# Cross-attention and a ternary feed-forward block on one core: single PE transposes between long matmuls in place of blocks of four and eight

## The chip, the core and the metric

The kernel is one program on one core of a Trainium2 chip. It has five engines with a queue each: TensorE (PE: matmuls, and PEld, its weight loads), VectorE (DVE), ScalarE (ACT), GpSimd (POOL) and SyncE (SP, which only issues DMAs here). An engine runs its queue in the order in which the program lists it. The metric is the time of one execution on the device in microseconds (us); lower is better.

## The reference

Eight sequences of 256 tokens with 512 features go through two residual blocks. What is computed, cut to what matters:

```python
q, k, v = heads(layernorm(x) @ Wq.T + bq), heads(ctx @ Wk.T + bk), heads(ctx @ Wv.T + bv)   # 16 heads of 32
q1, k1 = relu(q @ Wqf.T), relu(k @ Wkf.T) * mask            # 64 features for each head
out = (q1 @ (k1.T @ v)) / (q1 @ k1.sum(tokens) + 1e-8)      # linear attention
x = x + out @ Wo.T + bo
y = layernorm(x)                                            # int8-like rounding by row: bit_linear
a = bit_linear(y, w_up) * relu(bit_linear(y, w_gate)) ** 2  # ternary weights, 512 -> 2048
x = x + bit_linear(rmsnorm(a) * g, w_down)                  # 2048 -> 512
```

## The kernel before, in words

Two kinds of tile are used. A sequence a (0 to 7) has two row tiles i = 2a and 2a+1 of 128 tokens each. The attention part is computed in pairs of numbers: a high part in the matmul format fp32r (`.hi`, written by ACT) and the rest as a low part (`.lo`, written by DVE), so each product takes three matmuls: high*high, high*low and low*high. The feed-forward part runs in bf16 on small integers.

First comes the context part: keys, values and features of all eight sequences, up to about 160 us. Then a loop over p = 0 to 5 with a = p+1 and n = p+2 interleaves the feed-forward of row tiles 2p and 2p+1 with the attention of sequence a and with the start of sequence n, and a word list, TAIL, does the same for the end. The work of one turn, in the order in which PE gets it:

- `s3(a)`: feature matmuls of the queries. `gate_up(i, h)`: 8 gate and 8 up matmuls of 128x512 in bf16 for one half of the hidden width. `down(i)`: 16 matmuls of 128x512 in bf16.
- `s4(a, t)`: the attention product, 24 small matmuls (`at`, 66 columns) for each of the two row tiles. `mix(main, side, lag, end)` deals these 48 small ones out between the long matmuls of `gate_up` and `down`. It leaves the first `lag` and the last `end` long ones alone. Where there are more small ones than gaps, some gaps get two or more.
- `s5(a, t)`: the normalised attention output of a row tile (in `xn`) is transposed on PE: four fp32 transposes of 128x128, named `oT`, through a PSUM bank. ACT copies the high part into `qoh`, DVE the low part into `qol`. For t = 0 this stands in the side list of `mix` as one entry, for t = 1 behind the mix.
- `s6(a, t)`: the output projection of a row tile, 12 matmuls of 128x512 (`pr`, reading `qoh` or `qol` and `woh` or `wol`), then by DVE the residual sum (`x1`) and the layernorm statistics, then rounding (`xm`, `am`, `xq`), and a DMA that transposes the rounded tile into `xqT`, which `gate_up` of that tile reads in the next turn.
- `s1(n, t)`: four PE transposes of the normalised input of the next sequence (`xT`); ACT writes the high part into `aph` (`xT.hi`), DVE the low part into `apl` (`xT.lo`). `s2(n)`: 48 query matmuls of 128x256 that read `aph` and `apl` of both row tiles. The first of them waits for both `xT.lo`.

Only PE's order is written by hand. `Plan.queues` sorts the queues of ACT, DVE, POOL and SP: it runs through the program with a table of costs, and each free engine takes the open step with the smallest of (due time, need); a step's need is reckoned back from PE's order. So another order on PE also gives other orders on ACT, DVE, POOL and SP. Nothing is reordered on the chip: an ACT or DVE instruction waits behind what stands ahead of it.

The lines that matter: L338 emits all matmuls, L589 the transposes, L341 the ACT operations, L344 and L350 DVE operations. In `ps<-woh,qoh` the first name behind the arrow is the streamed operand and the second the loaded one.

Of the kernel before, what the change touches and what calls it, by code (L numbers as in the profile page):

```python
# [224 lines left out]
def xattn_bitffn_kernel(nc, x_d, ctx_d, wk_d, wv_d, wq_d, wo_d, feat_d, small_d, bv_d, bo_d, g_d, wg_d, wu_d, wd_d, out_d):  # L225
# [4 lines left out]
    with ExitStack() as es:  # L230
# [354 lines left out]
        def transposes(tag, t, waits):  # L585
            b = bank()
            for kc in range(KC):
                out, src = ps[:, b, P * kc:P * kc + P], xn[:, t, P * kc:P * kc + P]
                add("pe", f"{tag}.{kc}", 0.11, (waits + bank_user[b] + ["small"]) if kc == 0 else [], lambda e, out=out, src=src: e.transpose(out, src, eye))  # L589
            return b, f"{tag}.3"  # L590

        def s1(a, t):
            i = 2 * a + t
            b, k = transposes(f"xT{i}", t, [f"xn{i}"])
            src = ps[:, b, :].rearrange("p (a c) -> p a c", a=KC)

# [96 lines left out]
        def s5(a, t):  # L693
            i = 2 * a + t
            tt("pool", f"xbo{i}", 1.23, [f"xn{i}", "bo"], xs[:, i, :], xs[:, i, :], bo_b[:, :], ALU.add)
            b, k = transposes(f"oT{i}", t, [f"on{i}.0", f"on{i}.1"])
            cs = slice(512 * t, 512 * t + 512)
            act(f"oT{i}.hi", 0.5, [k], qoh[:, cs], ps[:, b, :], ACT.Copy)
            bank_user[b] = [tt("dve", f"oT{i}.lo", 0.62, [k, f"oT{i}.hi"], qol[:, cs], ps[:, b, :], f32(qoh[:, cs]), ALU.subtract)]
# [4 lines left out]
        def s6(a, t):  # L704
            i = 2 * a + t
            b = bank()
            for kc in range(KC):
                cs = slice(512 * t + P * kc, 512 * t + P * kc + P)
                waits = [f"oT{i}.lo"] + Wo_lo + bank_user[b] if kc == 0 else []
                k = products(f"pr{i}.{kc}", 0.2138, waits, ps[:, b, :], (qoh[:, cs], qol[:, cs]), (woh[:, kc, :], wol[:, kc, :]), kc == 0, kc == KC - 1)  # L710
            bank_user[b] = [tt("dve", f"x1.{i}", 0.62, [k, f"xbo{i}"], xs[:, i, :], ps[:, b, :], xs[:, i, :], ALU.add)]
# [185 lines left out]
        s6(0, 0)  # L897
        s1(1, 0)
        s1(1, 1)
        s6(0, 1)  # L900
        s2(1)
        kv_blocks(1)

# [102 lines left out]
```

How the kernel before makes its waits and increments, by code:

```python
        def run(lane, eng):  # L194
            seen = {}
            for i in order.get(lane, []):
                _, name, _, waits, fn, dma = self.steps[i]
                need = {}
                for w in waits:
                    s, v = at[w]
                    if need.get(s, (0, None))[0] < v:
                        need[s] = (v, w)
                for s, (v, _) in need.items():
                    if seen.get(s, 0) < v:
                        eng.wait_ge(s, v)
                        seen[s] = v
                last = fn(eng)
                if dma is not None:
                    last.then_inc(dma_sems[dma], 16)
                elif name in at:
                    last.then_inc(sems[lane], 1)
# [6 lines left out]
        def sync(e):  # L218
            run("sp", e)
            e.wait_ge(dma_sems["out"], issued["out"])
```

## Time and profile before

| | us |
|---|---|
| median of 3 runs (lowest, highest) | 475.62 (475.36, 476.45) |
| the profiled execution | 473.81 |
| its span, first to last instruction | 472.0 |
| PE busy | 460.8 (98%) |
| DVE busy | 359.2 (76%) |
| ACT busy | 301.9 (64%) |
| POOL busy | 178.5 (38%) |

PE is busy through nearly the whole span. The recorded time of a matmul runs from its dispatch to its last result, so neighbours overlap in the record: what a matmul costs is read from start to start, not from its duration. Of a small matmul behind a long one the start is recorded early. The granted TensorE clock is full in all 40 slices of the page.

### The profile page before, as it was taken

The numbers are of one execution on the slowest core, as the hardware profiler recorded it, in microseconds if no ns is written. First come the engines' busy times: TensorE is split into PE (matmuls) and PEld (weight loads), VectorE is DVE, ScalarE is ACT, GpSimd is POOL, SyncE is SP. The second block draws the span as 40 slices with busy tenths as digits, with TensorE's granted clock in tenths as the row PEclk, the third lists the DMA queues.
The fourth block names the chain that finished last, engine by engine and source line by source line (L and its number), as shares of the span: only waits on it lengthen the run. The fifth ranks groups of instructions, "written<-read, shape, count | busy, mean of one in ns | idle before, by whom it ended". The sixth has DMA issues, their size and how long they took to land.

```text
span 472.0 us, 7966 instructions
## 1 busy us (share of the span) xinstructions
PE 460.8 (98%) x3059; PEld 367.9 (78%) x3059; DVE 359.2 (76%) x638; ACT 301.9 (64%) x441; POOL 178.5 (38%) x310
## 2 busy tenths in 40 slices
PE   8999999999999999999999999999999999998996
PEld 6899999999899997885786876777678678684443
DVE  4835658538994696897788789789779799878782
ACT  5682888638133327768578567684866686747991
POOL 0000000001530164753654646466364563553750
PEclk9999999999999999999999999999999999999999
DMA  8971463703600120015015113203301320432044
GB/s 258 422 313 44 177 226 110 292 1 115 242 2 0 31 83 22 3 44 135 24 44 124 35 44 80 62 19 81 98 24 44 90 46 10 114 78 58 12 111 135
DMA packets 53078, 45.49 MB, mean 96 GB/s; under 512 B 43440, under 2 KB 44336, under 8 KB 51120
## 3 DMA queue, kind: packets, MB, share of 16 engines
q1 hardware_dynamic: 53040, 44.98, 30.5%
q8 instruction: 24, 0.39, 0.4%
q14 instruction: 14, 0.11, 0.1%
HBM read 27.14 MB, written 4.19 MB: 66 GB/s over the span
## 4 chain that ended last, share of the span: by engine, by line
PE 73%; POOL 6%; DVE 6%; ACT 5%; DMA 4%; issue 3%; SPq 2%; POOLq 0%; DVEq 0%; ACTq 0%
PE ps L338 71%; POOL zb L344 3%; PE ps L589 2%; ACT rb L341 2%; DMA xs<-in_wq_dram 2%; SPq L335 2%; DMA xqT<-xqb 2%; DVE zb L344 1%; ACT zb L341 1%; POOL tk L344 1%; POOL tk L347 1%; DMA yqTq<-yqb 1%; DVE yqb L792 1%; POOL zbe L344 1%; POOL xs L344 0%
## 5 line engine op out<-in xcount | busy, mean ns | idle before, releaser
L344 POOL TENSOR_TENSOR zb<-zb,g_b 128x1024 f32<-128x1024 f32 x28 | 67.2, 2400 | 61.2 <-ACT rb L341 43.9
L338 PE MATMUL ps<-tg,xqT 128*128 128x512 bf16 x256 | 68.1, 385 | 2.8 <-DMA xqT<-xqb 2.7
L338 PE MATMUL ps<-tu,xqT 128*128 128x512 bf16 x256 | 68.2, 385 | 0.0
L341 ACT ACTIVATE qoh<-ps,small 128x256 fp32r<-128x256 f32 x64 | 27.9, 468 | 40.1 <-PE ps L338 40.0
L338 PE MATMUL ps<-td,yqT 128*128 128x512 bf16 x208 | 50.7, 384 | 0.0
L341 ACT ACTIVATE rb<-zb 128x1024 f32<-128x1024 f32 x29 | 30.7, 1059 | 25.3 <-DVE zb L344 25.1
L341 ACT ACTIVATE rb<-ps 128x1024 f32<-128x1024 f32 x29 | 29.6, 1022 | 24.8 <-PE ps L338 23.8
L344 DVE TENSOR_TENSOR zb<-ps,rb 128x1024 f32<-128x1024 f32 x29 | 35.2, 1215 | 12.3 <-ACT rb L341 7.0
L341 ACT ACTIVATE zb<-zb,cm,tk 128x1024 f32<-128x1024 f32 x29 | 34.8, 1237 | 13.7 <-POOL tk L344 13.7
L338 PEld LDWEIGHTS ps<-tg,xqT 128*128 128x128 bf16 x256 | 23.8, 99 | 23.7 <-issue 2.9
L338 PEld LDWEIGHTS ps<-tu,xqT 128*128 128x128 bf16 x256 | 25.1, 99 | 21.5
L338 PE MATMUL ps<-kvh,apl 128*128 128x66 f32 x112 | 41.1, 367 | 0.0
L347 POOL TENSOR_SCALAR tk<-tk 128x1 f32<-128x1 f32 x96 | 30.7, 321 | 27.1 <-DVE tk L716 19.8
L338 PE MATMUL ps<-kvh,aph 128*128 128x66 f32 x112 | 40.2, 359 | 0.7 <-DVE apl L350 0.7
L338 PE MATMUL ps<-kvl,aph 128*128 128x66 f32 x112 | 40.4, 361 | 0.0
L765 DVE TENSOR_REDUCE tk<-zb 128x1 f32<-128x1024 f32 x30 | 36.3, 1210 | 3.3 <-POOL zb L344 3.2
L350 DVE SCALAR_TENSOR_TENSOR qol<-ps,small,qoh 128x256 fp32r<-128x256 f32 x64 | 27.9, 475 | 13.1 <-ACT qoh L341 12.9
L338 PE MATMUL ps<-aph,wkh 128*128 128x256 f32 x128 | 35.7, 283 | 0.7 <-DVE kp L347 0.7
L338 PE MATMUL ps<-aph,wqh 128*128 128x256 f32 x128 | 36.0, 281 | 0.1
L338 PE MATMUL ps<-apl,wqh 128*128 128x256 f32 x128 | 35.9, 280 | 0.0
L338 PE MATMUL ps<-aph,wql 128*128 128x256 f32 x128 | 35.9, 280 | 0.0
L338 PE MATMUL ps<-apl,wkh 128*128 128x256 f32 x128 | 35.3, 280 | 0.0
(153 smaller groups left out, 1357.0 us busy)
## 6 DMA issues: line engine op xcount, KB each, us to landing
xs<-in_wg_dram SPq DMA_DIRECT2D x4, 1024.0 KB, 13.4
xs<-in_wu_dram SPq DMA_DIRECT2D x4, 1024.0 KB, 5.3
xs<-in_wd_dram SPq DMA_DIRECT2D x4, 1024.0 KB, 9.3
xs<-in_x_dram SPq DMA_DIRECT2D x8, 512.0 KB, 4.1
out_dram<-xs SPq DMA_DIRECT2D x15, 256.0 KB, 2.0
craw<-in_ctx_dram SPq DMA_DIRECT2D x7, 512.0 KB, 7.4
qoh<-qol SPq DMA_DIRECT2D x12, 128.0 KB, 2.3
qy<-qol SPq DMA_DIRECT2D x12, 128.0 KB, 2.3
```

Source lines behind the costliest of these rows:

```text
L335: return add("sp", name, 2.9 * mb, waits, lambda e: e.dma_start(out, in_), sem)
L338: return add("pe", name, cost, waits, lambda e: e.matmul(out, lhsT, rhs, start=start, stop=stop))
L341: return add("act", name, cost, waits, lambda e: e.activation(out, in_, func, **kw))
L344: return add(lane, name, cost, waits, lambda e: e.tensor_tensor(out, a, b, op))
L347: return add(lane, name, cost, waits, lambda e: e.tensor_scalar(out, a, s1, s2, op0, op1))
L350: return add("dve", name, cost, waits, lambda e: e.scalar_tensor_tensor(out, a, s, b, op0, op1))
L589: add("pe", f"{tag}.{kc}", 0.11, (waits + bank_user[b] + ["small"]) if kc == 0 else [], lambda e, out=out, src=src: e.transpose(out, src, ...
L765: add("dve", f"ym{u}", 1.15, [f"Y{u}"], lambda e: e.tensor_reduce(col(M0 + h, i), zs, AX_X, ALU.max, apply_absolute_value=True))
L792: add("dve", f"yb{v}", 0.6, [f"yk{v}"] + war, lambda e, dst=dst, z=z: e.tensor_scalar(dst, z, MAGIC, None, ALU.subtract))
```

## The change

`transposes`, `s1`, `s5` and `s6` no longer emit their PE work at once: each gives back a list of calls, one for each transpose or matmul, with the copies and the row work behind the last one. The lists are dealt out by `mix`:

- The four transposes of `s5(a, 0)` are four entries in the side list of the attention products, where one entry stood before (52 in place of 49).
- In the loop the four transposes of `s1(n, 0)` are dealt out between the 12 projections of `s6(a, 0)`, and those of `s1(n, 1)` between the first five projections of `s6(a, 1)`.
- `s5(a, 1)`, and all of the sequences 0 and 1 ahead of the loop, keep their order. No instruction is added or left out.

```diff
-        def transposes(tag, t, waits):
-            b = bank()
+        def transposes(tag, t, waits, evict):
+            calls = []
+            cell = {}
             for kc in range(KC):
+                def call(kc=kc):
+                    if kc == 0:
+                        cell["b"] = bank()
+                    b = cell["b"]
...
+                    add("pe", f"{tag}.{kc}", 0.11, (waits + bank_user[b] + ["small"]) if kc == 0 else [], lambda e: e.transpose(out, src, eye))
+                    if kc == KC - 1:
+                        evict(b, f"{tag}.{kc}")
+                calls.append(call)
+            return calls
...
             side = s4(a, 0) + s4(a, 1)
-            side.insert(36, lambda: s5(a, 0))
+            side[36:36] = s5(a, 0)
             main = gate_up(2 * p, 1) + (down(2 * p - 1) if 0 < p < NB - 3 else []) + gate_up(2 * p + 1, 0) + gate_up(2 * p + 1, 1)
             mix(main, side, 6, 10)
-            s5(a, 1)
+            mix(s5(a, 1), [])
             ln1(n)
-            s6(a, 0)
-            s1(n, 0)
-            s1(n, 1)
-            s6(a, 1)
+            mix(s6(a, 0), s1(n, 0), 1, 3)
+            mix(s6(a, 1), s1(n, 1), 0, 8)
             s2(n)
...
                 side = s4(a, 0) + s4(a, 1)
-                side.insert(36, lambda: s5(a, 0))
+                side[36:36] = s5(a, 0)
                 mix(sum([part(w) for w in r.split(",")], []), side, 6, 10)
```

First place: PE between the bf16 matmuls, in the turn p = 4 (the list is `s4(5)` with `s5(5, 0)` in it). `tg`, `tu` mark gate and up matmuls, `kvh` and `kvl` the attention products, `small,xn` the transposes. Before:

```order
L338 MATMUL ps<-kvl,aph 128x66
L338 MATMUL ps<-tu,xqT 128x512
L338 MATMUL ps<-kvh,apl 128x66
L338 MATMUL ps<-tu,xqT 128x512
L589 MATMUL ps<-small,xn 128x128 x4
L338 MATMUL ps<-tu,xqT 128x512
L338 MATMUL ps<-kvh,aph 128x66
```

and in the changed kernel:

```order
L338 MATMUL ps<-tg,xqT 128x512
L595 MATMUL ps<-small,xn 128x128
L338 MATMUL ps<-tu,xqT 128x512
L595 MATMUL ps<-small,xn 128x128
L338 MATMUL ps<-tu,xqT 128x512
L595 MATMUL ps<-small,xn 128x128
L338 MATMUL ps<-tu,xqT 128x512
L595 MATMUL ps<-small,xn 128x128
L338 MATMUL ps<-kvh,aph 128x66
L338 MATMUL ps<-tu,xqT 128x512
```

Each transpose takes a gap of its own, or the first place of one, and the attention products that stood in these gaps move to others.

Second place: PE in the output projections of the same turn (`woh`, `wol`: `pr`). Before there were 12 projections, eight transposes and 12 projections; the rows around the eight:

```order
L338 MATMUL ps<-woh,qoh 128x512
L338 MATMUL ps<-wol,qoh 128x512
L338 MATMUL ps<-woh,qol 128x512
L589 MATMUL ps<-small,xn 128x128 x8
L338 MATMUL ps<-woh,qoh 128x512
```

In the changed kernel, from the first projection of the second row tile on:

```order
L338 MATMUL ps<-woh,qoh 128x512
L595 MATMUL ps<-small,xn 128x128
L338 MATMUL ps<-wol,qoh 128x512
L595 MATMUL ps<-small,xn 128x128
L338 MATMUL ps<-woh,qol 128x512
L595 MATMUL ps<-small,xn 128x128
L338 MATMUL ps<-woh,qoh 128x512
L595 MATMUL ps<-small,xn 128x128
L338 MATMUL ps<-wol,qoh 128x512
```

Behind the last transpose of the turn stood 12 projections ahead of the query matmuls; now there are 8.

Third place: DVE in the last turn of the loop (n = 7). `apl<-ps,aph` is `xT.lo`, `xs<-ps,xs` is `x1`, `yqb<-zb` a rounding of the feed-forward, `zb<-ps,rb` its product of up and gate, `st`, `mv` the statistics. Before:

```order
L344 TENSOR_TENSOR kvl<-kvc,kvh 64x8x33
L344 TENSOR_TENSOR xs<-ps,xs 128x512
L344 TENSOR_TENSOR apl<-ps,aph 128x4x128 x2
L573 BN_STATS st<-xs 128x6
L574 BN_AGGR mv<-st 128x2
```

and in the changed kernel:

```order
L344 TENSOR_TENSOR apl<-ps,aph 128x4x128
L344 TENSOR_TENSOR xs<-ps,xs 128x512
L573 BN_STATS st<-xs 128x6
L574 BN_AGGR mv<-st 128x2
L818 TENSOR_SCALAR yqb<-zb 128x1024
L344 TENSOR_TENSOR zb<-ps,rb 128x1024
L344 TENSOR_TENSOR apl<-ps,aph 128x4x128
```

On ACT, in the same place, the two `xT.hi` stood together; now two scalings of the feed-forward (`zb<-zb,cm,tk`, named `yk`) stand between them:

```order
L341 ACTIVATE aph<-ps 128x4x128
L341 ACTIVATE zb<-zb,cm,tk 128x1024 x2
L341 ACTIVATE aph<-ps 128x4x128
```

In the turns n = 3 to 6 the order between the two `xT.lo` on DVE is `x1` and two roundings, and on ACT between the two `xT.hi` one `yk` and one `kvh`.

## Rows read from the trace of the kernel before

**Rows 1.** The page: busy time, share of the span, instructions

```profile
PE 460.8 (98%) x3059; PEld 367.9 (78%) x3059; DVE 359.2 (76%) x638; ACT 301.9 (64%) x441; POOL 178.5 (38%) x310
```

**Rows 2.** Waits of PE: engine, line, releaser: total us, times, longest

```profile
PE ps L338 <- DMA xqT<-xqb: 2.7, 3, 1.3
...
PE ps L338 <- DVE apl L350: 0.7, 1, 0.7
```

**Rows 3.** Timeline of PE around an `oT` block: start us, us, engine, line, operation

```profile
210.54 3.63 PE L338 MATMUL ps<-td,yqT 128*128 128x512 bf16 x16
...
230.65 0.39 PE L338 MATMUL ps<-tg,xqT 128*128 128x512 bf16 x1
230.69 0.38 PE L338 MATMUL ps<-kvl,aph 128*128 128x66 f32 x1
230.91 0.39 PE L338 MATMUL ps<-tu,xqT 128*128 128x512 bf16 x1
...
231.17 0.39 PE L338 MATMUL ps<-tu,xqT 128*128 128x512 bf16 x1
231.40 0.60 PE L589 MATMUL ps<-small,xn 128*128 128x128 f32 x4
231.84 0.38 PE L338 MATMUL ps<-tu,xqT 128*128 128x512 bf16 x1
```

**Rows 4.** Timeline of the weight loads in the same place

```profile
230.64 0.10 PEld L338 LDWEIGHTS ps<-tg,xqT 128*128 128x128 bf16 x1
...
231.73 0.10 PEld L338 LDWEIGHTS ps<-tu,xqT 128*128 128x128 bf16 x1
```

**Rows 5.** Timeline of PE: two attention products in one gap

```profile
187.33 0.39 PE L338 MATMUL ps<-tu,xqT 128*128 128x512 bf16 x1
187.37 0.38 PE L338 MATMUL ps<-kvh,apl 128*128 128x66 f32 x1
187.59 0.28 PE L338 MATMUL ps<-kvh,aph 128*128 128x66 f32 x1
187.70 0.39 PE L338 MATMUL ps<-tu,xqT 128*128 128x512 bf16 x1
```

**Rows 6.** The transposes' line: ns min/median/max, first and last start

```profile
L589 PE MATMUL ps<-small,xn x128: 270/273/303, 137.0 to 421.1; 128*128 128x128 f32 x128
```

**Rows 7.** Timeline of PE, the projections of the turn n = 7

```profile
388.28 0.48 PE L338 MATMUL ps<-woh,qoh 128*128 128x512 f32 x1
...
390.87 0.40 PE L338 MATMUL ps<-woh,qol 128*128 128x512 f32 x1
...
391.11 1.03 PE L589 MATMUL ps<-small,xn 128*128 128x128 f32 x8
...
392.21 0.40 PE L338 MATMUL ps<-wol,qoh 128*128 128x512 f32 x1
...
394.72 0.28 PE L338 MATMUL ps<-aph,wqh 128*128 128x256 f32 x1
```

**Rows 8.** The same stretch on ACT and POOL

```profile
391.74 1.09 ACT L341 ACTIVATE aph<-ps 128x512 fp32r<-128x512 f32 x2 [1.34 <-PE ps L589]
...
391.97 0.19 POOL L344 TENSOR_TENSOR tk<-sy,tk 128x1 f32<-128x1 f32 x1
...
392.72 2.38 ACT L341 ACTIVATE zb<-zb,cm,tk 128x1024 f32<-128x1024 f32 x2
```

**Rows 9.** The same stretch on DVE

```profile
391.31 0.69 DVE L344 TENSOR_TENSOR xs<-ps,xs 128x512 f32<-128x512 f32 x1 [0.44 <-PE ps L338]
...
392.45 1.29 DVE L344 TENSOR_TENSOR apl<-ps,aph 128x512 fp32r<-128x512 f32 x2 [0.45 <-ACT aph L341]
...
393.65 0.68 DVE L573 BATCH_NORM_STATS2 st<-xs 128x6 f32<-128x512 f32 x1
...
394.37 0.18 DVE L574 BATCH_NORM_AGGREGATE mv<-st 128x2 f32<-128x6 f32 x1
394.47 0.67 DVE L792 TENSOR_SCALAR yqb<-zb 128x1024 bf16<-128x1024 f32 x1
...
397.06 1.21 DVE L344 TENSOR_TENSOR zb<-ps,rb 128x1024 f32<-128x1024 f32 x1
```

More of the change, by code:

```diff
@@ L695, in s5, with evict @@
             tt("pool", f"xbo{i}", 1.23, [f"xn{i}", "bo"], xs[:, i, :], xs[:, i, :], bo_b[:, :], ALU.add)
[L696 to L699, printed above, removed]
+            def evict(b, k):
+                cs = slice(512 * t, 512 * t + 512)
+                act(f"oT{i}.hi", 0.5, [k], qoh[:, cs], ps[:, b, :], ACT.Copy)
+                bank_user[b] = [tt("dve", f"oT{i}.lo", 0.62, [k, f"oT{i}.hi"], qol[:, cs], ps[:, b, :], f32(qoh[:, cs]), ALU.subtract)]
+            return transposes(f"oT{i}", t, [f"on{i}.0", f"on{i}.1"], evict)
         def col(k, i):
@@ L705, in s6 @@
             i = 2 * a + t
-            b = bank()
+            calls = []
+            cell = {}
             for kc in range(KC):
[L708 to L711, printed above, removed]
@@ L718, in s6 @@
-            recip(f"sx{i}", 0.07, [f"sxi{i}"], col(SX, i), col(SXI, i))
-            act(f"xq{i}.m", 0.7, [f"sx{i}", f"am{i}", f"xm{i}", "cm0"], xq32[:, :], xq32[:, :], ACT.Identity, scale=col(SX, i), bias=cm[:, 0:1])
-            war = [f"xqT{i - 1}"] if i else [end1]
-            add("dve", f"xq{i}.b", 0.34, [f"xq{i}.m"] + war, lambda e: e.tensor_scalar(xqb[:, :], xq32[:, :], MAGIC, None, ALU.subtract))
-            war = [f"U{i - 3}.1"] if i > 2 else [end1]
-            add("sp", f"xqT{i}", 0.4, [f"xq{i}.b"] + war, lambda e: e.dma_start_transpose(xqT[:, i % 3, :, :], xqb[:, :]), f"xqT{i % 3}")
@@ L724, in s6, with call @@
-            ts("pool", f"sx3{i}", 0.35, [f"sxi{i}"], col(SX3, i), col(SXI, i), col(SXI, i), col(SXI, i), ALU.mult, ALU.mult)
-            tt("pool", f"cc{i}", 0.15, [f"sx3{i}", "CW"], col(CC, i), col(SX3, i), CW, ALU.mult)
-            ts("pool", f"c2{i}", 0.25, [f"cc{i}"], col(C2, i), col(CC, i), col(CC, i), 1.0 / FI, ALU.mult, ALU.mult)
+                for z in range(3):
+                    def call(kc=kc, z=z):
+                        waits = []
+                        if kc == z == 0:
+                            cell["b"] = bank()
+                            waits = [f"oT{i}.lo"] + Wo_lo + bank_user[cell["b"]]
+                        b = cell["b"]
+                        cs = slice(512 * t + P * kc, 512 * t + P * kc + P)
+                        left, right = qol if z == 2 else qoh, wol if z == 1 else woh
+                        k = mm(f"pr{i}.{kc}.{z}", 0.2138, waits, ps[:, b, :], left[:, cs], right[:, kc, :], kc == z == 0, kc == KC - 1 and z == 2)
+                        if kc == KC - 1 and z == 2:
+                            rows(b, k)
+                    calls.append(call)
@@ L729, in gate_up @@
+            return calls
         def gate_up(i, h):
@@ L873, in xattn_bitffn_kernel @@
         mix(kv(last - 1), [])
-        s1(0, 0)
-        s1(0, 1)
+        mix(s1(0, 0) + s1(0, 1), [])
         kv_blocks(0)
```

50 lines of the change are left out of this document (28 added, 22 removed).

## The prediction, made before the changed kernel was run

> **What bounds the kernel now.** I began with the busy table of the page: PE is busy for 460.8 of 472.0 us, the next engine, DVE, for 76% [rows 1]. So nearly every nanosecond that PE's queue gains or loses reaches the end, and an engine beside it matters only where PE waits for it. Then I read the waits of PE: 2.7 us in three waits for a transposed tile `xqT`, one of 0.7 us for `apl` [rows 2]. The rest is some waits at the start and in the tail. Last came the timeline around the transposes, from start to start, since the records of neighbours overlap.
>
> **What one PE operation costs, before.** A long bf16 matmul alone: sixteen in a row take 3.63 us, the last 0.38, so (3.63 - 0.38) / 15 = 0.217 us [rows 3]. With one attention product in the gap the next long one starts 0.26 us later (230.65 to 230.91), so a lone product costs 0.045 [rows 3]. With two in the gap it is 187.33 to 187.70, 0.37 us, so the second costs 0.11 [rows 5]: 0.065 more than in a gap of its own. Four transposes in one gap: 231.17 to 231.84 is 0.67, less 0.217 makes 0.45, or 0.113 each [rows 3]. Eight between projections: 390.87 to 392.21 is 1.34; a projection costs (394.72 - 392.21) / 11 = 0.228, two of them 0.456, which leaves 0.88 or 0.11 each [rows 7].
>
> **What a lone transpose costs** is the first question, for no row shows one. It could be as cheap as a lone product (0.045) if the 0.11 in a block were only its weight load, which a long matmul ahead would hide. Against it: behind the last transpose of the block the next bf16 load begins at 231.73 and its matmul starts 0.11 later, at 231.84, while elsewhere such a matmul starts 0.01 behind the begin of its load (230.64, 230.65) [rows 3, 4]. So what holds it is not the load but the transpose, which takes its 0.11 itself. Its record says so too: every transpose lasts about 273 ns [rows 6], as long as a matmul with 256 columns (0.28) [rows 7], though it has 128. I take 0.11 for a lone one, the same as in a block. The ends for the range: 0.045, the lone product, and 0.126, if each change from a long matmul costs the 0.013 that lie between 231.17 + 0.217 and 231.40. In PE's order the transposes that stand right behind another one fall from 105 to 45, so 60 become lone: they bring between 60 x (0.045 - 0.113) = -4.1 and 60 x 0.013 = +0.8 us; I take 0.
>
> The Trainium skill, page "TensorE: Matmul & The Clock Gate", sections "LDWEIGHTS (loading the stationary operand)" and "Back-to-back issue gap", has a rule that speaks for a gain: a load takes the number of its columns over 1.2, here 107 ns, and the matmul itself N/2.4 + 2.5, here 56 ns, so a transpose whose load is hidden would cost 56. As an estimate by that page, only those right ahead of a bf16 matmul would profit, since a projection's own 107 ns load follows the others; they grow by 11, which makes -0.6 us. The 107 agrees with the 0.11 in a block [rows 3]; the 56 does not go with the rows on the last transpose [rows 3, 4], and the rows decide.
>
> **Step 1, the attention mix.** The four calls of `s5(a, 0)` do not find free gaps. `mix` uses every gap anyway (48 in the turns p = 1 to 4, 32 in p = 0 and 5, 24 in the tail), and the list grows from 49 to 52. A transpose now takes a gap in which a product stood, and the product becomes the second in another gap. In PE's order the products right behind another product rise from 96 to 107: 11 x 0.065 = +0.7 us, all on PE's path. This is the price of lone transposes where the gaps are full.
>
> **Step 2, projections with `xT` between.** PE's own cost: nothing, 0.11 each in both orders. No query matmul moves, since the sum of work ahead of it is the same. What moves is the cover. The queries wait for `xT.lo` of both tiles. Before, 12 projections stood behind the last transpose: 12 x 0.228 = 2.7 us for two `hi` and two `lo`. Now it is 8: 1.82 us. The chain that must fit: from a transpose's start to ACT 0.30 (391.11 + 3 x 0.11 = 391.44, ACT starts at 391.74), `hi` 0.55, a hand-over of 0.1 to 0.2, `lo` 0.65 [rows 7 to 9], in all 1.65 to 1.7 against 0.11 + 1.82 = 1.93 from that start. With both engines free 0.2 us are spare. But they are not free: the new orders put feed-forward work between the two tiles' copies.
>
> The turn n = 7, laid out with the old durations from the first projection at 388.28 [rows 7 to 9]: the last transpose of the first tile starts behind 8 projections, 388.28 + 8 x 0.235 + 3 x 0.11 = 390.5 (0.235 is 390.87 less 388.28, over 11), its `hi` runs 390.8 to 391.4. Then ACT has the two scalings, which wait for POOL (391.97 + 0.19) and take 2.38: 392.2 to 394.55. So the second `hi` runs to 395.1, although its transposes (start 394.72 - 1.93 = 392.8) were ready at 393.1. On DVE the first `lo` ends at 392.25, then `x1` 0.69, statistics 0.68 and 0.18, `yqb` 0.67 end at about 394.4, the 1.21 of `zb<-ps,rb` at 395.6, the second `lo` at 396.25. The queries start at 396.3 in place of 394.72: +1.5 us of PE waiting. Behind the late copies stand `xm` and the rest of the row's chain, and behind the queries all of PE.
>
> The turns n = 3 to 6, counted from their first projection: first `lo` 3.3 to 3.95, `x1` to 4.6, two `yqb` to 5.95, second `lo` to 6.6 and queries at 6.65, where 394.72 - 388.28 = 6.44 is their place: 0.2 each. On ACT one scaling (1.19) and a `kvh` fit between the `hi`. If one of the 1.2 us operations of DVE is just running, it is more; I take 0.3 each, 4 x 0.3 = +1.2. Ends: 0 and 1.2 each. In the turn n = 2 such a loss disappears in the wait for `xqT` that follows [rows 2].
>
> **Step 3, the row chain to `xqT`.** The first tile's projections end 4 x 0.11 = 0.44 later, and the statistics stand behind the second `lo`. The wait for `xqT` at the head of the next turn grows where it was there already, once in the middle of the loop: +0.3. Against it, PE's wait of 0.7 us for `apl` [rows 2] takes up as much of what came shortly ahead: -0.7.
>
> **Step 4, everything else.** The copies of `oT` have the same cover: a turn's mix goes on for 16 long matmuls behind the first tile, and the second keeps its block. DMAs: the same, none moved past another of its queue on SP, nothing for POOL but neighbours exchanged. Cost 0.
>
> **Sum.** 0 + 0.7 + 1.5 + 1.2 + 0.3 - 0.7 = +3.0 us, on the profiled execution's 473.81: 476.8. The median of the runs shown is 475.62, 1.8 above it, and I add the same 3.0: 478.6 us.
>
> **Rivals.**
> 1. Cheap lone transposes: 0.045 in place of 0.11. -4.1 + 3.0 = -1.1: 474.5, faster. For it: the attention products do just that [rows 3]. Against it: rows 4 and 6. It decides as soon as a lone one costs under 0.065, where 60 of them outweigh 3.0. Chance 0.08.
> 2. The new orders help: with `R` and its square ahead of the second `oT.hi`, or other exchanges, PE's wait for `apl` (0.7) and one or two of those for `xqT` (about 1.4 of 2.7) go [rows 2], and no new one comes. 0.7 - 2.1 = -1.4: 474.2. Against it: these waits hang on long chains over three engines with a later start. Chance 0.09.
> 3. No new waits, the sorting has laid the copies well: only step 1 stays, +0.7: 476.3. For it: `Plan.queues` reckons the needs from the new PE order. Against it: its queue for n = 7, as laid out. Chance 0.13.
> 4. The cover is too thin in every turn: another 0.5 us for each of n = 2 to 7: +6.0: 481.6. For it: 0.2 us of slack and DVE at 76%. Chance 0.09.
> 5. The forecast, +1.5 to +4.5: 477.1 to 480.1. Chance 0.61.
>
> **Chances and range.** About 0.2% (0.95 us) is what a measurement of this kernel can tell from no change. Faster: rivals 1 and 2, 0.17. Within it: most of rival 3 and a little of the others, 0.14. Slower: 0.69. The range 474.9 to 481.5 leaves out about 0.1 below and 0.07 above.
>
> **What would show it.** In the changed profile: a lone transpose between bf16 matmuls makes their distance 0.33 (right) or 0.26 (rival 1). Two projections with one transpose between them stand 0.34 apart. A new wait of PE for `apl` ahead of the first `wqh` matmul of a turn, largest in n = 7, about 1.5 us; none there makes steps 2 and the sum wrong, and leaves rival 3. The wait for `xqT` at the head of a turn should not shrink by more than PE's own delay; if it does, rival 2. PE's busy time should rise by 0.7 at most.

## The result and the profile after

The changed kernel takes 481.25 us (median of 6 runs, 480.03 to 483.26); the kernel before, on the same chip, 476.03 (6 runs, 475.36 to 477.25). The ratio is 1.0114 with a 95% interval of 1.0087 to 1.0141: slower by 5.2 us, where +3.0 was forecast. The median lies inside the range that was given, near its upper end. About half of the executions of the kernel before have a mean granted clock of 0.996 in place of 1.000 and take some 2 us more (medians of 477.0 to 477.2 against 474.9 to 475.1 us in the three sessions of the experiments), so the table below also gives the difference among executions at full clock alone.

The page of the changed kernel, in the columns of [rows 1]:

```profile
span 479.1 us, 7961 instructions
...
PE 462.4 (97%) x3059; PEld 365.2 (76%) x3059; DVE 365.4 (76%) x638; ACT 302.8 (63%) x441; POOL 183.0 (38%) x310
```

The span grew by 7.1 us over 472.0, but PE's busy time only by 1.6 (462.4 over 460.8). Most of the loss is therefore idle time of PE. The list of its waits (total us, times, longest) says for whom:

```profile
PE ps L338 <- DVE apl L350: 4.0, 4, 1.1
PE ps L338 <- DMA yqTq<-yqb: 2.5, 1, 2.5
PE ps L338 <- DMA xqT<-xqb: 2.4, 4, 1.3
PE ps L338 <- DVE apl L344: 1.8, 2, 1.3
```

Against [rows 2] there are two new things. The wait for `apl` from L344 (`xT.lo`, ahead of the queries) is the one that was forecast. The wait for `apl` from L350 grew from 0.7 in one piece to 4.0 in four, and it is the larger. In that row `apl` holds the low part of the attention's features, and PE waits at the first attention product of a turn. The last wait for `yqTq` stands in the tail, behind the last transposed tile of the feed-forward. It is 2.5 here and between 0.9 and 2.8 in most of the profiled executions below, in no order that follows the edits, so I leave it out. In four of those executions (the two single sides, PE after, POOL early) the granted clock also fell to half for 3.4 us in this tail, between 466 and 476 us. What remains is read from the first transpose to the last, a stretch that holds the whole loop. It was 421.1 - 137.0 = 284.1 us [rows 6] and is now 426.9 - 136.9 = 290.0:

```profile
L595 PE MATMUL ps<-small,xn x128: 270/272/321, 136.9 to 426.9; 128*128 128x128 f32 x128
```

That is +5.9, and I call this stretch the loop in all that follows. It is taken from one profiled execution per kernel.

**A lone transpose.** First the timeline of PE in the changed kernel where [rows 3] had the block of four, then its weight loads (start us, us):

```profile
231.35 0.39 PE L338 MATMUL ps<-tg,xqT 128*128 128x512 bf16 x1
231.58 0.27 PE L595 MATMUL ps<-small,xn 128*128 128x128 f32 x1
231.69 0.38 PE L338 MATMUL ps<-tu,xqT 128*128 128x512 bf16 x1
231.91 0.27 PE L595 MATMUL ps<-small,xn 128*128 128x128 f32 x1
232.02 0.38 PE L338 MATMUL ps<-tu,xqT 128*128 128x512 bf16 x1
```

```profile
231.36 0.14 PEld L595 LDWEIGHTS ps<-small,xn 128*128 128x128 f32 x1
231.58 0.10 PEld L338 LDWEIGHTS ps<-tu,xqT 128*128 128x128 bf16 x1
```

The load of the transpose begins with the long matmul ahead and is over at 231.50, 0.08 before the transpose starts; it is hidden. Still the next long matmul starts 0.11 behind the transpose (231.58 to 231.69), and two long ones with one transpose between stand 0.33 apart (231.69 to 232.02). So the 0.11 is not the wait for its load but the transpose's own time. The estimate by the Trainium skill, page "TensorE: Matmul & The Clock Gate", section "Back-to-back issue gap" (N/2.4 + 2.5, 56 ns here) does not hold for this fp32 transpose; the measured 0.11 decides.

**The turn n = 7.** PE, ACT and DVE of the changed kernel, as in [rows 7 to 9]:

```profile
392.28 0.48 PE L338 MATMUL ps<-woh,qoh 128*128 128x512 f32 x1
...
396.52 0.27 PE L595 MATMUL ps<-small,xn 128*128 128x128 f32 x1
...
396.86 0.27 PE L595 MATMUL ps<-small,xn 128*128 128x128 f32 x1
...
398.57 0.39 PE L338 MATMUL ps<-woh,qol 128*128 128x512 f32 x1
400.30 0.38 PE L338 MATMUL ps<-aph,wqh 128*128 128x256 f32 x1 [1.34 <-DVE apl L344]
```

```profile
395.89 2.38 ACT L341 ACTIVATE zb<-zb,cm,tk 128x1024 f32<-128x1024 f32 x2 [0.43 <-POOL tk L344]
398.18 0.57 ACT L341 ACTIVATE aph<-ps 128x512 fp32r<-128x512 f32 x1
```

```profile
397.71 0.68 DVE L818 TENSOR_SCALAR yqb<-zb 128x1024 bf16<-128x1024 f32 x1
398.42 1.23 DVE L344 TENSOR_TENSOR zb<-ps,rb 128x1024 f32<-128x1024 f32 x1
399.56 0.68 DVE L344 TENSOR_TENSOR apl<-ps,aph 128x512 fp32r<-128x512 f32 x1
```

The queries start 8.02 behind the first projection (400.30 - 392.28), where 8.0 was laid out and 6.44 stood before. The cause is the one that was laid out too: ACT's two scalings stand between the two `hi`, DVE's product of up and gate ahead of the second `lo`. Two projections with a transpose between them are 0.34 apart (396.52 to 396.86).

**The new wait.** PE of the changed kernel in the turn n = 3 (the first attention product of the mix that follows), and what POOL did shortly before:

```profile
261.85 0.30 PE L338 MATMUL ps<-kvh,aph 128*128 128x66 f32 x1 [0.80 <-DVE apl L350]
```

```profile
247.87 0.24 POOL L347 TENSOR_SCALAR tk<-tk 128x1 f32<-128x1 f32 x1 [1.45 <-DVE tk L742]
248.07 2.42 POOL L344 TENSOR_TENSOR zb<-zb,g_b 128x1024 f32<-128x1024 f32 x1
...
252.26 0.19 POOL L347 TENSOR_SCALAR lnv<-mv 128x1 f32<-128x1 f32 x1
252.53 0.55 POOL L344 TENSOR_TENSOR rstd<-lnv,cm 128x1 f32<-128x1 f32 x1
253.08 0.34 POOL L347 TENSOR_SCALAR tk<-tk 128x1 f32<-128x1 f32 x1
253.50 0.19 POOL L344 TENSOR_TENSOR tk<-tk,wst 128x1 f32<-128x1 f32 x1
253.80 1.19 POOL L347 TENSOR_SCALAR tk<-tk 128x1 f32<-128x1 f32 x3
...
255.27 0.19 POOL L344 TENSOR_TENSOR tk<-sy,tk 128x1 f32<-128x1 f32 x1
```

The same place in the kernel before:

```profile
245.60 0.24 POOL L347 TENSOR_SCALAR tk<-tk 128x1 f32<-128x1 f32 x1 [1.45 <-DVE tk L716]
245.81 2.42 POOL L344 TENSOR_TENSOR zb<-zb,g_b 128x1024 f32<-128x1024 f32 x1
...
251.95 0.19 POOL L344 TENSOR_TENSOR tk<-sy,tk 128x1 f32<-128x1 f32 x1
252.09 0.56 POOL L344 TENSOR_TENSOR rstd<-lnv,cm 128x1 f32<-128x1 f32 x1
```

`tk<-sy,tk` is `kk`, the factor of the feed-forward's rounding in a row tile. ACT's scalings `yk` need it, and behind them in ACT's queue stand `R` and its square, the feed-forward's next steps, and then the high parts of the features, `aph`, on which DVE's `apl` rests. So one small step on POOL sets when the attention may begin. `kk` comes 3.3 us later than before, PE at this place only about 0.9. Two things delay it. The long POOL step `zb<-zb,g_b` starts 2.26 later (1.65 of it counted from the turn's first projection): in both kernels a scale of the row chain stands ahead of it in POOL's queue, and that row's statistics now stand behind the second copy `xT.lo` on DVE. And from its end to `kk` it takes 4.78 in place of 3.72, because five small steps of the other tile (`lnv`, `rstd`, and the three that make `sx3`, `cc`, `c2`) now all stand ahead of it; before, two of them did (`lnv` and `sx`), and `rstd`, `cc` and `c2` stood behind.

From `kk` to the first attention product it is 261.85 - 255.27 = 6.58. In the kernel before, the same order on POOL occurs in one turn, n = 5, and that is the turn of its one wait of 0.7:

```profile
330.57 0.19 POOL L344 TENSOR_TENSOR tk<-sy,tk 128x1 f32<-128x1 f32 x1
```

```profile
337.15 0.30 PE L338 MATMUL ps<-kvh,aph 128*128 128x66 f32 x1 [0.75 <-DVE apl L350]
```

337.15 - 330.57 is 6.58 again. Where `kk` came earlier (251.95 + 6.58 = 258.53), PE arrived at 259.88 and did not wait.

PE's own rows do not show all of such a wait. The record of the matmul ahead still runs for part of it, while the weight load of the waiting product shows it in full. For this copy the weight loads of the kernel before wait 1.9 us in four turns, and those of the changed kernel:

```profile
PEld ps L338 <- DVE apl L350: 5.9, 4, 1.6
```

In the turn n = 2 the new wait only takes another's place. Before, PE had waited for `xqT` there:

```profile
215.22 1.89 PE L338 MATMUL ps<-tg,xqT 128*128 128x512 bf16 x8 [1.05 <-DMA xqT<-xqb]
```

Now this wait is gone, PE comes 0.86 early to that point, and 7 us later it waits 1.09 for `apl` at 222.47.

### The profile page after: what moved, and what is told of

It is laid out like the page before. It is cut to its first block, busy times and chain, and to the rows that moved or that the text cites. A ratio compares the mean times of both kernels' runs of the same rounds, so it can differ in the third digit from the quotient of the medians.

```text
span 479.1 us, 7961 instructions
## 1 busy us (share of the span) xinstructions
PE 462.4 (97%) x3059; PEld 365.2 (76%) x3059; DVE 365.4 (76%) x638; ACT 302.8 (63%) x441; POOL 183.0 (38%) x310
## 4 chain that ended last, share of the span: by engine, by line
PE 54%; DVE 15%; POOL 10%; ACT 7%; issue 6%; DMA 5%; SPq 1%; DVEq 0%; POOLq 0%; ACTq 0%
PE ps L338 52%; POOL zb L344 3%; ACT rb L341 3%; POOL tk L347 2%; DMA xqT<-xqb 2%; POOL tk L344 2%; ACT zb L341 2%; DMA xs<-in_wq_dram 2%; PE ps L595 2%; DVE zb L344 2%; DVE st L573 2%; DVE apl L344 2%; SPq L335 1%; DVE yqb L818 1%; ACT aph L341 1%
## 5 line engine op out<-in xcount | busy, mean ns | idle before, releaser
L344 POOL TENSOR_TENSOR zb<-zb,g_b 128x1024 f32<-128x1024 f32 x28 | 67.4, 2409 | 54.9 <-DVE apl L350 22.9
L338 PE MATMUL ps<-tg,xqT 128*128 128x512 bf16 x256 | 68.1, 385 | 2.4 <-DMA xqT<-xqb 2.4
L338 PE MATMUL ps<-tu,xqT 128*128 128x512 bf16 x256 | 68.8, 384 | 0.0
L338 PE MATMUL ps<-td,yqT 128*128 128x512 bf16 x208 | 51.7, 384 | 0.0
L347 POOL TENSOR_SCALAR tk<-tk 128x1 f32<-128x1 f32 x96 | 34.1, 356 | 34.0 <-DVE tk L742 22.4
L338 PE MATMUL ps<-kvh,aph 128*128 128x66 f32 x112 | 39.4, 352 | 4.0 <-DVE apl L350 4.0
L344 DVE TENSOR_TENSOR zb<-ps,rb 128x1024 f32<-128x1024 f32 x29 | 35.3, 1218 | 9.7 <-ACT rb L341 8.3
L338 PEld LDWEIGHTS ps<-tu,xqT 128*128 128x128 bf16 x256 | 25.1, 99 | 21.8 <-DVE zb L344 0.3
L338 PEld LDWEIGHTS ps<-tg,xqT 128*128 128x128 bf16 x256 | 23.9, 99 | 22.9 <-issue 2.3
L338 PE MATMUL ps<-kvl,aph 128*128 128x66 f32 x112 | 40.2, 359 | 0.0
L338 PE MATMUL ps<-kvh,apl 128*128 128x66 f32 x112 | 40.1, 358 | 0.0
L338 PE MATMUL ps<-aph,wqh 128*128 128x256 f32 x128 | 36.2, 283 | 1.8 <-DVE apl L344 1.8
L350 DVE SCALAR_TENSOR_TENSOR qol<-ps,small,qoh 128x256 fp32r<-128x256 f32 x64 | 27.7, 473 | 12.9 <-ACT qoh L341 12.9
L338 PE MATMUL ps<-aph,wkh 128*128 128x256 f32 x128 | 35.8, 284 | 0.5 <-DVE kp L347 0.5
L338 PE MATMUL ps<-aph,wql 128*128 128x256 f32 x128 | 35.6, 278 | 0.0
L338 PE MATMUL ps<-apl,wqh 128*128 128x256 f32 x128 | 35.6, 278 | 0.0
L338 PE MATMUL ps<-apl,wkh 128*128 128x256 f32 x128 | 35.3, 279 | 0.0
```

Of the source, the lines that this page charges most:

```text
L338: return add("pe", name, cost, waits, lambda e: e.matmul(out, lhsT, rhs, start=start, stop=stop))
L344: return add(lane, name, cost, waits, lambda e: e.tensor_tensor(out, a, b, op))
L347: return add(lane, name, cost, waits, lambda e: e.tensor_scalar(out, a, s1, s2, op0, op1))
L350: return add("dve", name, cost, waits, lambda e: e.scalar_tensor_tensor(out, a, s, b, op0, op1))
```

## The experiments

Two theories. The cover, which is the forecast's mechanism (A in the expectations): the loss comes from PE's order itself, since 8 projections behind the last transpose cover less than 12. The queues (B): it comes from the orders of ACT, DVE and POOL, which are sorted anew around PE's. Within the queues, two culprits were tried one after the other: the place of ACT's scalings `yk` (called C in the expectations) and POOL's small steps ahead of `kk` (called D).

In most kernels the orders were frozen, so that one queue could be changed alone. The lists of ACT, DVE, POOL and SP are given as names:

```diff
-        order = self.queues()
+        order = {"pe": [i for i, s in enumerate(self.steps) if s[0] == "pe"]}
+        for lane, names in ORDER.items():
+            order[lane] = [self.index[w] for w in names.split()]
```

This shifts line numbers: L344 reads L384 or L385, L350 reads L390 or L391, L338 reads L378 or L379. All kernels ran in 5 rounds, in three sessions, each beside the kernel before; a ratio is to the kernel before of the same session. Loop is the stretch from first to last transpose, less the 284.1 of before. "Full clock" is the median of the executions at a mean granted clock of 0.999 or more, less the same of the kernel before; how many there were stands in brackets. For the changed kernel the 475.1 of the first session is taken. Executions of one kernel at full clock still spread over some 2 us, so differences under about 0.8 are not clear of noise there.

| kernel | median us (runs) | ratio, 95% interval | full clock | loop | waits for `xT.lo` / features / `xqT` |
|---|---|---|---|---|---|
| before | 476.03 (6) | 1 | 0 | 0 | 0 / 0.7 / 2.7 |
| changed | 481.25 (6) | 1.0114, 1.0087 to 1.0141 | +5.5 (4) | +5.9 | 1.8 / 4.0 / 2.4 |
| attention side only | 478.75 (12) | 1.0065, 1.0040 to 1.0089 | +2.8 (7) | +4.3 | 0 / 4.1 / 2.2 |
| projection side only | 479.25 (6) | 1.0073, 1.0047 to 1.0099 | +4.1 (3) | +4.5 | 0.6 / 3.8 / 0.8 |
| PE after, rest before | 478.08 (12) | 1.0045, 1.0022 to 1.0069 | +2.1 (8) | +3.0 | 0 / 1.7 / 3.8 |
| PE before, rest after | 486.66 (6) | 1.0220, 1.0189 to 1.0251 | +9.7 (1) | +10.7 | 6.0 / 4.0 / 1.9 |
| lone `xT`, 12 behind | 479.05 (9) | 1.0055, 1.0033 to 1.0077 | +2.3 (4) | +3.0 | 0.6 / 1.2 / 3.8 |
| changed, `yk` early | 484.46 (6) | 1.0153, 1.0124 to 1.0183 | +6.6 (2) | +7.2 | 1.8 / 4.9 / 1.6 |
| the same, and n = 7 | 486.48 (6) | 1.0208, 1.0172 to 1.0244 | +8.0 (1) | +8.6 | 0.5 / 4.6 / 5.1 |
| before, `yk` early, n = 5 | 475.16 (12) | 0.9975, 0.9955 to 0.9995 | -0.3 (9) | -0.3 | 0 / 0.7 / 2.6 |
| changed, POOL's order | 479.20 (11) | 1.0064, 1.0042 to 1.0087 | +3.1 (6) | +3.8 | 1.8 / 1.1 / 2.5 |
| the same, and n = 7 | 482.85 (6) | 1.0135, 1.0107 to 1.0164 | none | +7.0 | 0.5 / 1.5 / 4.6 |
| before, POOL late | 478.26 (12) | 1.0037, 1.0018 to 1.0057 | +3.2 (10) | +2.7 | 0 / 2.3 / 2.8 |
| before, POOL early, n = 5 | 474.87 (12) | 0.9970, 0.9946 to 0.9994 | -0.5 (7) | -0.7 | 0 / 0.3 / 2.8 |

In the profiled executions of two kernels the granted clock fell to half inside the loop, for 3.4 us: of "PE before, rest after" at 405.35, right behind a wait of PE of 2.3 us, and of "POOL's order, and n = 7" at 410.69, behind a wait of 2.7. The query matmuls of the first then start 0.21 apart in place of 0.12. This makes some 1.6 us of the +10.7 and of the +7.0. The turn n = 7 of "`yk` early, and n = 7" had a wait of 3.2 without such a fall.

### One side of the change at a time

Only the attention side (the block of eight `xT` restored):

```diff
-            mix(s6(a, 0), s1(n, 0), 1, 3)
-            mix(s6(a, 1), s1(n, 1), 0, 8)
+            mix(s6(a, 0) + s1(n, 0) + s1(n, 1) + s6(a, 1), [])
```

> Only the attention side is changed: the four transposes of the first row tile are single entries of the side list, while the transposes of the next x stand as a block of eight between the projections as before; the planner sorts the other queues anew. Theory A (the loss comes from PE's own order: second attention products in a gap, and the thin cover behind the last transpose of x): the cover is back at 12 projections, so only the 11 extra second products stay, 0.7 us: ratio 1.001 to 1.002, no wait of PE for apl at the head of the query matmuls. Theory B (the loss comes from the newly sorted queues of ACT, DVE and POOL, which make PE wait about 1 us for the feature copies at the first attention product of a turn): those waits stay as large as in the changed kernel, 4 us in four, and the ratio is 1.007 to 1.009.

Only the projection side (the block of four `oT` restored):

```diff
-            side[36:36] = s5(a, 0)
+            side.insert(36, lambda: mix(s5(a, 0), []))
```

> Only the projection side is changed: single transposes of the next x between the projections, with the attention output's transposes as one block of four; the planner sorts the other queues anew. Theory A: all of the waits at the query matmuls (0.2 us in most turns, 1.3 in the last) and none of the second products: +2 to +2.5 us, ratio 1.004 to 1.005. Theory B: the waits at the first attention product stay too: +4.5 to +5, ratio 1.009 to 1.011.

The waits of the two, attention side first:

```profile
PE ps L338 <- DVE apl L350: 4.1, 4, 1.1
```

```profile
PE ps L338 <- DVE apl L350: 3.8, 4, 1.3
...
PE ps L338 <- DVE apl L344: 0.6, 1, 0.6
```

Without any `xT` between projections the queries are back at 6.44 behind the first projection and the wait for `xT.lo` is gone: that part is the projection side's, as forecast. But the four waits for the features are there with either side alone, at 4.1 and 3.8. So neither the thin cover nor the mix alone makes them, which leaves the queues that either edit sorts anew; the cross below tests that. It also shows why the parts don't add up: +4.3 and +4.5 in the loop against +5.9 for both. Both ratios, 1.0065 and 1.0073, lie above theory A's and a little below theory B's.

With the projection side only, POOL's order ahead of `kk` in n = 3 to 5 is the one that the kernel before has in n = 4, and the waits are there all the same. POOL's order is thus not their only source.

### PE's order and the others', crossed

PE's order of the changed kernel with the other queues of before (the frozen lists of before), and the reverse:

> PE's order is that of the changed kernel, while ACT, DVE, POOL and SyncE keep the order of the kernel before, written into the program as a list. Theory A: the loss is PE's order, so it stays: ratio 1.009 to 1.012. Theory B: what is left is 0.7 us for the second products and little at the query matmuls, since the two copies of x stand together: ratio 1.001 to 1.003. If single transposes were of use at all, this kernel would be at or below 1.0.

> The reverse: PE's order is that of the kernel before, and ACT, DVE, POOL and SyncE have the order of the changed kernel, written in as a list. Theory A: back to 1.000 to 1.003, since the cover is 12 projections again. Theory B: the waits at the first attention product come with the queues alone, and in the last turn of the loop the second copy of x still stands behind two scalings and a product: +4 to +5 us, ratio 1.008 to 1.011.

With PE's new order alone the loop is 3.0 longer, and the ratio of 1.0045 lies between the two theories; the other 2.9 of the 5.9 come when the queues are sorted to it. This is no clean division, since the two sides depend on each other. The wait for `xT.lo` does not occur at all here: in before's queues the second copy stands early enough even for 8 projections. What was read as thin cover is thus a matter of the queues too. The reverse cross answers the question about the features: with PE's order untouched, the new queues alone bring the 4.0 us in four waits. It is the slowest of all, at 1.0220, outside both theories' ranges, with the wait for `xT.lo` at

```profile
PE ps L379 <- DVE apl L385: 6.0, 6, 2.3
```

Under the order of PE that they were not sorted for, the new queues cost 10.7 us, 1.6 of it the clock, against 5.9 for the whole change.

### Lone transposes with the full cover

PE's order of before and its other queues, but the eight `xT` singly between the twelve projections of the first tile, with the twelve of the second behind them:

```diff
+            mix(s6(a, 0), s1(n, 0) + s1(n, 1), 1, 2)
+            mix(s6(a, 1), [])
```

> PE as in the kernel before, with one difference: the eight transposes of the next x stand singly between the 12 projections of the first row tile, so 12 projections of cover stay behind them; the attention output is transposed in blocks of four. ACT, DVE, POOL and SyncE keep the order of the kernel before. This prices a lone transpose: if it costs what one in a block costs, the distance from the first projection to the first query matmul stays 6.44 us or grows by 0.1 (8 x 0.01), ratio 0.999 to 1.002. If a lone one were cheap (0.045 in place of 0.11), the distance falls to 5.9 and the ratio to about 0.994.

In the turns n = 5 and 7 the queries stand 6.50 and 6.51 behind the first projection, against 6.44 with the block: 0.06 over eight transposes, under 0.01 each. In the other turns small waits stand in between (6.62 to 6.75, in n = 2 7.22). A lone transpose costs what one in a block does, here too. The loop is 3.0 longer all the same, and the ratio of 1.0055 misses the expected 0.999 to 1.002. The first tile's last projection comes up to 8 x 0.11 = 0.88 later, and the waits for `xqT`, for the features and for `xT.lo` are 2.2 longer together than before.

### First culprit: the scalings `yk`

In the changed kernel, n = 3, 4 and 5, ACT's two `yk` were moved ahead of the copy `oT.hi`, `R` and its square, with `sy`, `kk` and the roundings that belong to them (and `ym` on DVE, which they displace):

```diff
 ACT (n = 3)
  zz6
+ yk4
+ yk5
+ oT5.hi
  R7
  RR7
- oT5.hi
  kvh3.odd
- yk4
  xT6.hi
- yk5
```

> The changed kernel with its own PE order and its own queues, but in the turns n = 3, 4 and 5 ACT runs the two scalings yk ahead of R, its square and the second oT.hi, as the kernel before has it in n = 3 and 4; what they wait for (sy on DVE, kk on POOL) and the roundings behind them (yb) move with them. Theory C (late scalings push the roundings between the copies of x on DVE, these push the statistics and the product Z, then Y on POOL, the next kk and the next pair of scalings, and R behind these is late, so the feature copies and with them PE's first attention product): the waits of PE for apl in L350 fall from 4.0 us to about 1 (only the first turn keeps its own), ratio to the kernel before 1.004 to 1.007. Rival (the waits come from PE's order, singles and thin cover): they stay at 3 to 4 us and the ratio at 1.010 to 1.012.

The features' wait did not fall but rose to 4.9 from 4.0:

```profile
PE ps L379 <- DVE apl L391: 4.9, 4, 1.3
```

Theory C is refuted. The same move in the kernel before, in its one turn with the wait:

> The kernel before, PE untouched, with one turn's queues changed: in n = 5, the only turn of it that has the late scalings, they are moved ahead as in its turns n = 3 and 4. Theory C: its wait of 0.75 us at the first attention product of the next turn goes, ratio 0.998 to 0.999, within the noise, but visible in the trace. Rival: the wait is independent of this and stays.

The wait is still 0.7, and the loop is 0.3 shorter; C fails here as well. Its ratio of 0.9975 has an interval just below 1, but 9 of its 12 executions ran at full clock and only 7 of the 20 of the kernel before. Among those at full clock the difference is -0.3 us, within noise.

### The turn n = 7

Added to the kernel with `yk` early: the second `hi` right behind the first, the second `lo` behind the statistics.

```diff
 ACT (n = 7)
  xT14.hi
+ xT15.hi
  yk20
  yk21
- xT15.hi
 DVE (n = 7)
  ln1.12.agg
+ xT15.lo
  yb20
  Z23
- xT15.lo
```

> As the kernel with early scalings, and besides in the last turn of the loop the two copies of x stand together again: xT15.hi right behind xT14.hi on ACT, xT15.lo ahead of yb and Z on DVE. The layout of the prediction says that the 1.3 us wait at the query matmuls of this turn comes from what stands between, not from the 8 projections of cover: it falls to under 0.3, ratio 1.001 to 1.004. If the thin cover itself is the cause, at least 1 us of wait stays there.

The query wait of 1.3 in n = 7 is gone, and the next wait for `xqT`, which was 0.44 at that place, is now

```profile
413.33 1.89 PE L379 MATMUL ps<-tg,xqT 128*128 128x512 bf16 x8 [3.23 <-DMA xqT<-xqb]
```

The wait moved and grew, and the ratio of 1.0208 is far from the expected 1.001 to 1.004. The traces show the way. On ACT the second `hi` now waits for its transposes, ahead of the scalings:

```profile
399.39 0.60 ACT L382 ACTIVATE aph<-ps 128x512 fp32r<-128x512 f32 x1 [1.71 <-PE ps L636]
```

Counted from the turn's first projection, the scalings start at 5.38 in place of 3.59. On DVE the product of up and gate starts at 7.38 in place of 6.15, and POOL's long step `zb<-zb,g_b` at 9.93 in place of 8.70. The scale of the row chain stands behind that step (12.40 in place of 11.19), and the rounded tile is ready for its DMA 1.2 later. PE's next tile starts 1.3 later in all, though its queries come 1.5 earlier. A milder form, `xT15.hi` between the two `yk`, on top of POOL's order of the next part, did the same, with one wait for `xqT` of 2.7:

> As the kernel with POOL's order mended, and besides in the last turn of the loop the second xT.hi stands between the two scalings on ACT and the second xT.lo ahead of the rounding and the product on DVE. By the layout of the prediction the second lo then ends about 6.6 us behind the first projection: the wait for apl in L344 falls from 1.3 to about 0.2 us, while one scaling comes 0.6 later. If this wait only moves, as with both copies together, the wait for xqT behind it grows by as much. Ratio 1.002 to 1.005 if it does not.

So the late second copy in n = 7 can't simply be undone: both earlier places that were tried cost more in the row chain than they save at the queries. In the milder form the wait for `xqT` grew by 2.1, more than the 1.3 saved, and 1.6 of its loop are the fall of the clock.

### Second culprit: POOL's small steps

In the changed kernel, POOL alone, in n = 3, 4 and 5:

```diff
 POOL (n = 3)
  crs3
+ mx3
+ syi3
+ so3
+ kk3
  ln1.5.var
  ln1.5.rstd
  sx34
  cc4
  c24
- mx3
- syi3
- so3
- kk3
```

> The changed kernel, PE, ACT, DVE and SyncE as they are; only POOL's queue is changed, in the turns n = 3, 4 and 5: the four small steps that end in kk (mx, syi, so, kk), on which the next pair of scalings and R behind them wait, stand ahead of the five small steps of the attention row tiles (variance, rstd, sx3, cc, c2), not behind them. Theory D (the waits of PE at the first attention product come through kk, late by those five steps, about 1.2 us): the waits for apl in L350 fall from 4.0 to about 1 us, and the ratio from 1.011 to 1.005. Rival (they come from the statistics behind the second copy of x, ahead of Y on POOL): they stay at 3 us or more.

The waits, and the same place on POOL:

```profile
PE ps L378 <- DVE apl L384: 1.8, 2, 1.3
...
PE ps L378 <- DVE apl L390: 1.1, 1, 1.1
```

```profile
249.51 2.42 POOL L384 TENSOR_TENSOR zb<-zb,g_b 128x1024 f32<-128x1024 f32 x1
...
255.99 0.19 POOL L384 TENSOR_TENSOR tk<-sy,tk 128x1 f32<-128x1 f32 x1 [0.22 <-DVE sy L393]
256.26 0.19 POOL L387 TENSOR_SCALAR lnv<-mv 128x1 f32<-128x1 f32 x1
```

```profile
223.91 0.30 PE L378 MATMUL ps<-kvh,aph 128*128 128x66 f32 x1 [1.10 <-DVE apl L390]
...
262.56 0.30 PE L378 MATMUL ps<-kvh,aph 128*128 128x66 f32 x1
```

In PE's own rows the three waits in the three altered turns are gone, and the one in the turn n = 2, which was not altered, stands as it was. From the end of the long step to `kk` it is 4.06 in place of 4.78. But the weight loads show that the waits became shorter and did not end:

```profile
PEld ps L378 <- DVE apl L390: 3.3, 4, 1.6
```

```profile
262.56 0.19 PEld L378 LDWEIGHTS ps<-kvh,aph 128*128 128x128 f32 x1 [0.57 <-DVE apl L390]
```

The product still starts 6.57 to 6.58 behind `kk` in all three turns, so the chain still sets its time. The loop is 2.1 shorter than in the changed kernel, and the two ratios' intervals meet only at 1.0087; at full clock the medians are 480.6 and 478.0. Nothing but the place of four small steps on an engine that is 38% busy was changed.

The reverse, in the kernel before: POOL's late order in n = 3 and 4, and the early one in n = 5.

> The reverse: the kernel before, with POOL's order of the changed kernel in the turns n = 3 and 4 alone (the five small steps of the row tiles ahead of the four that end in kk). In the trace of before the feature copies of these turns end 0.8 us or so ahead of need, and kk comes some 1.9 us later: theory D expects two new waits of PE for apl of about 1 us each at the first attention product, and a ratio of 1.003 to 1.005. The rival expects none, ratio 1.000.

> The kernel before with one change: on POOL in the turn n = 5, the only one of its turns 3 to 5 that has the five small steps ahead of the four that end in kk, the four go first. Theory D: its wait of 0.7 us for apl goes, at the first attention product of the next turn, and the ratio is 0.998 to 0.9995. The rival: the wait stays at 0.7.

The late order brought a wait of 1.33 where there was none:

```profile
300.41 0.30 PE L379 MATMUL ps<-kvh,aph 128*128 128x66 f32 x1 [1.33 <-DVE apl L391]
```

and made the loop 2.7 longer, the whole kernel by 0.37%, or by 3.2 us (0.67%) among executions at full clock. In n = 3, PE's rows show no wait. There `kk` came 1.44 later (253.39 against 251.95), the weight load waits 0.43 and the product comes 0.7 later behind its first gate matmul. Theory D expected about 1 us in each of the two turns. In n = 4 `kk` came 2.0 later, counted from the turn's first projection, and most of that is not the small steps' own time: the first of the five waits for the second tile's statistics on DVE, and the four that end in `kk` stand behind it.

```profile
290.84 0.19 POOL L388 TENSOR_SCALAR lnv<-mv 128x1 f32<-128x1 f32 x1 [1.78 <-DVE mv L615]
```

The early order in n = 5 cut that wait to 0.29:

```profile
337.19 0.30 PE L379 MATMUL ps<-kvh,aph 128*128 128x66 f32 x1 [0.29 <-DVE apl L391]
```

Its `kk` starts at 330.61, 6.58 ahead. This kernel has the lowest median of all, 0.9970 of before (0.9946 to 0.9994). Its loop is 0.7 shorter, 0.15%; at full clock the difference is -0.5 us, which agrees with the loop but is not clear of noise. The trace shows the shorter wait; the ratio by itself does not show a gain, since the kernel with `yk` early, whose wait did not change, measured nearly the same.

## Why the forecast was right in direction and short in size

By its own steps, from the places of the same instructions in the two profiled executions:

| step | forecast | measured |
|---|---|---|
| own cost of lone transposes | 0 | 0 (0.11 each, as in a block) |
| step 1, attention mix | +0.7 | +0.5 |
| step 2, n = 2 | 0 | +0.4 |
| step 2, n = 3 to 6 | +1.2 | +0.7 (4 x 0.17) |
| step 2, n = 7 | +1.5 | +1.6 |
| step 3, `xqT` and `apl` | -0.4 | +2.7 |

- **The lone transpose.** Right, and shown three times: 0.33 apart between bf16 matmuls, 0.34 between projections, and 6.50 for 6.44 with the full cover. Rival 1 is refuted. The step that carried most of the chance of "faster" was decided rightly by the last transpose of the block in [rows 3, 4].
- **Step 1.** Right in size (0.5 for 0.7). PE's busy time rose by 1.6, though, where 0.7 at most was named as the sign; no run shows what the rest is. That the gaps were full was the point: the mix had no free places.
- **Step 2.** Right. In n = 3 to 6 the queries came at 6.61 to 6.62, 0.2 late was laid out, 0.3 taken and 0.17 measured; the added 0.1 for a busy DVE was not needed. In n = 7 the layout hit 8.02 with 8.0. In n = 2 the queries came 0.4 later, and the wait for `xqT` behind them took it up, as forecast. The mechanism has one correction: with before's queues the thin cover costs next to nothing (the queries stand at 6.52 in n = 4 to 7, without a wait for `xT.lo`), so it is the orders around the copies that make the wait, and the layout from the new orders was what made the forecast good.
- **Step 3, the step that failed.** The forecast had +0.3 for the row chain and -0.7 for the wait for `apl`, which was to swallow delays of PE. From the queries to the first matmul on `xqT` PE gained 1.0 over all turns, 1.2 of it in n = 2, where the wait of 1.05 vanished. But from there to the first attention product it lost 1.4, 1.1, 1.2 and 0.3 in four turns and gained 0.2 in n = 7, 3.7 in all. The mistake was to take the one wait of 0.7 for a slack. It was the end of a chain from `kk`, 6.58 long, and had I read the chain back I would have found POOL's order of that turn at its head, and seen that the changed kernel has that order in every turn from n = 2 to 5.
- **Step 4.** "Nothing for POOL but neighbours exchanged. Cost 0" is the sentence that the POOL experiment refutes: exchanging neighbours cost 2.1 us of the loop in the changed kernel and 2.7 in the kernel before. The steps are 0.2 to 0.6 us long, but they stand ahead of one on which ACT, DVE and PE wait in turn, and where one of them waits itself, all behind it do.
- **Rival 4**, too thin a cover in every turn at +6.0, came near in number, but not by its mechanism: the waits at the queries that PE's rows show are 1.8 in two turns.

The terms as measured make the +5.9 of the loop; another 1.2 of the profiled difference of 7.1 is the tail's wait, which varies (2.48 against 1.25). The medians differ by 5.2, or by 5.5 at full clock. That the median lies in the range is in part luck: the range reached to 481.5 to take in most of rival 4, and 2.7 us came from a place that the forecast put at -0.4.

What stays open: with POOL's order mended the changed kernel is still 0.64% behind. Of its 3.8 us of loop, 0.6 are the mix and 2.7 the later queries, 1.6 of these in n = 7. The remaining 0.5 is the way from the queries to the first product. There the chain from `kk` still holds PE, in n = 3 and 4 by 0.35 and 0.24 beyond the kernel before, and the later place of the statistics is in it. It was not tried by itself, but the traces put a number on it: in the changed kernel and the two single sides POOL's long step starts 3.5 us behind the start of the first tile's statistics on DVE in all of n = 3 to 5, and in the kernel before in n = 4 and 5. In n = 3 these statistics start 6.48 us behind the turn's first projection in place of 3.75. Of the 2.7 us by which `kk` is later there, counted so, 1.65 lie ahead of the long step and 1.05 behind it.

## What to carry to other kernels

Where one engine is 97% busy and the others' queues are sorted around it, a change of its order is priced in two parts: what the moved instructions cost there, and what the resorted queues do at each of its waits. Here 3.0 of 5.9 us stood with PE's new order alone, and the rest came with the queues. For each wait of the bounding engine, however short, follow the chain to its head, and look in the new orders of every engine, the idle ones too, for what now stands ahead of that head. A wait removed by moving one step ahead in a full queue can come back elsewhere: twice here it came back larger. Look at the weight loads' waits beside PE's own, and compare like clock with like where a ratio is near 1.

## What the runs showed of the hardware

A fp32 transpose on PE holds it for 0.11 us even when its weight load is wholly hidden behind a bf16 matmul (load over at 231.50, transpose at 231.58, next matmul at 231.69). The lone attention product with 66 columns in the same place costs 0.045 [rows 3]. By these two rows the price of a small operation between long ones is not its load; that it goes by what streams is the likely reading, which two sizes alone do not prove.

The distance from `kk` on POOL over ACT and DVE to PE was 6.57 to 6.59 us at nine places where PE's rows show a wait there, in five kernels: beside the three above, 215.89 to 222.47, 294.61 to 301.20 and 333.98 to 340.56 in the changed one, 217.33 to 223.91 with POOL's order mended, and 293.84 to 300.41 and 332.99 to 339.57 with POOL late in the kernel before. It was 6.57 to 6.58 at the three altered turns with POOL's order mended, too, where only the weight load shows the wait. On a chain whose queues keep one order the hand-overs hardly varied here, and such a constant helped to find the chain.

The granted clock has fallen to half for 3.4 us at a time in several of these executions, behind waits of PE of 2 us or more in the two kernels where it fell inside the loop, and a wait of 3.2 us passed without it in another.
